# Layer 1 of a cross network in 19 matmul passes instead of 21, with VectorE's products at other places

## The reference, cut to what matters

```python
for W in filters:            # (39*39, 128), (39*128, 128), (39*128, 128)
    z = jnp.einsum('bfd,bgd->bfgd', x0, xk).reshape(b, f * g, d)
    cur = jnp.einsum('bpd,pm->bmd', z, W)
    outs.append(cur)
    xk = cur
z = jnp.sum(jnp.concatenate(outs, axis=1), axis=-1)    # (512, 384)
h = jnp.concatenate([z, dense_ctx], axis=1)
h = jnp.maximum(h @ W_top1 + b_top1, 0.0)
h = jnp.maximum(h @ W_top2 + b_top2, 0.0)
y = h @ W_top3
```

## Time and profile before

| | us |
|---|---|
| median of 2 runs (680.06 to 683.67) | 681.87 |
| the profiled execution, own time | 676.92 |
| its span, first to last instruction | 674.9 |
| busy in that span: TensorE matmul | 636.6 |
| VectorE | 565.5 |
| GpSimd | 533.3 |
| ScalarE | 374.1 |
| first matmul of layer 2 of tile 0 starts at | 45.27 |

### The profile page before, as it was taken

How to read it: one execution, slowest core, us unless ns; L and a number is a source line. 1 busy time by engine, 2 the same in 40 slices (tenths; PEclk the granted TensorE clock), 3 DMA queues, 4 the chain that set the end, 5 groups by cost and what they waited for, 6 DMA issues and landing times.

```text
span 674.9 us, 11454 instructions
## 1 busy us (share of the span) xinstructions
PE 636.6 (94%) x2900; PEld 504.6 (75%) x2900; DVE 565.5 (84%) x1934; ACT 374.1 (55%) x1129; POOL 533.3 (79%) x528
## 2 busy tenths in 40 slices
PE   3388999999999999999999999999999999999998
PEld 1256667777778788888878888888878888887867
DVE  4468888979899898989789898989879898988760
ACT  0445464646556574747467564746557474755431
POOL 6757879999999999998879999897969988574420
PEclk9999999999999999999999999999999999999989
DMA  9535642203241313113230322204031221200000
GB/s 185 112 70 140 211 117 68 62 6 89 40 110 18 98 29 81 44 29 95 43 85 8 84 44 66 60 10 113 10 88 37 63 62 41 81 0 1 2 0 1
DMA packets 79940, 42.25 MB, mean 63 GB/s; under 512 B 56721, under 2 KB 64721, under 8 KB 79746
## 3 DMA queue, kind: packets, MB, share of 16 engines
q1 hardware_dynamic: 67246, 35.85, 20.7%
q10 hardware_dynamic: 7380, 4.38, 3.2%
q0 software_dynamic: 5248, 1.29, 1.9%
HBM read 39.52 MB, written 1.94 MB: 61 GB/s over the span
## 4 chain that ended last, share of the span: by engine, by line
PE 68%; POOL 14%; DVE 5%; issue 5%; SPq 3%; ACT 2%; DMA 2%; POOLq 0%; DVEq 0%
PE y L900 16%; PE y L902 15%; PE y L901 15%; DVE scaled L802 4%; POOL emb_quads L481 4%; PE side L907 4%; PE late L918 4%; PE acc L882 3%; PE acc L877 3%; PE acc L876 3%; POOL sum L514 2%; POOL z_parts L499 2%; POOL sum L507 2%; ACT scaled L594 2%; PE y L918 2%
## 5 line engine op out<-in xcount | busy, mean ns | idle before, releaser
L802 DVE SCALAR_TENSOR_TENSOR scaled<-y,x_rows,scaled 128x128 f32<-128x128 f32 x1728 | 465.4, 341 | 63.4 <-ACT scaled L594 51.7
L594 ACT ACTIVATE scaled<-y,x_rows 128x128 f32<-128x128 f32 x768 | 218.9, 367 | 221.0 <-PE y L902 220.9
L900 PE MATMUL y<-w_hi,x_parts 128*128 128x512 f32 (+1 forms) x640 | 280.5, 438 | 9.5 <-DVE scaled L802 3.4
L902 PE MATMUL y<-w_hi,x_parts 128*128 128x512 f32 (+1 forms) x640 | 248.1, 388 | 0.0
L901 PE MATMUL y<-w_lo,x_parts 128*128 128x512 f32 (+1 forms) x640 | 247.6, 387 | 0.0
L481 POOL DMA_INDIRECT emb_quads<-in_small_tables_dram,quad_rows x144 | 139.2, 967 | 27.4 <-issue 15.6
L900 PEld LDWEIGHTS y<-w_hi,x_parts 128*128 128x128 f32 x640 | 120.6, 188 | 49.6 <-DVE scaled L802 23.0
L499 POOL TENSOR_TENSOR z_parts<-z,z_parts 117x512 fp32r<-117x512 f32 (+1 forms) x95 | 123.3, 1298 | 29.3 <-ACT z_parts L553 28.5
L902 PEld LDWEIGHTS y<-w_hi,x_parts 128*128 128x128 f32 x640 | 120.1, 188 | 24.9
L901 PEld LDWEIGHTS y<-w_lo,x_parts 128*128 128x128 f32 x640 | 121.0, 189 | 20.9 <-issue 2.6
L514 POOL TENSOR_TENSOR sum<-sum,scaled 128x512 f32<-128x512 f32 x63 | 81.7, 1296 | 26.5 <-DVE scaled L802 25.3
(11 more groups left out here) (94 smaller groups left out, 376.2 us busy)
## 6 DMA issues: line engine op xcount, KB each, us to landing
z<-x_turned SPq DMA_DIRECT2D x311, 78.0 KB
x_three<-x_turned SPq DMA_DIRECT2D x48, 78.0 KB
x_turned<-emb_quads SPq DMA_DIRECT2D x156, 8.0 KB
w_sb<-in_w_dram SPq DMA_DIRECT2D x1, 2496.0 KB, 9.6
emb_quads<-in_small_tables_dram,quad_rows POOLq DMA_INDIRECT x144, 2.4
s_sb<-in_w_dram ACTq DMA_DIRECT2D x12, 160.0 KB, 5.3
x_turned<-emb_singles SPq DMA_DIRECT2D x89, 2.0 KB
x_turned<-emb_quads SPq DMA_DIRECT2D x64, 2.0 KB
```

Source lines behind the costliest of these rows:

```text
L594: done = act.activation(scaled[:, k % 2, BY_ACT.index(j), i * M:(i + 1) * M], y2[n % RING][:, i * M:(i + 1) * M], ACT.Copy, scale=x0_rows[ ...
L802: dve.scalar_tensor_tensor(part, y2[n % RING][:, i * M:(i + 1) * M], x0_f, part, ALU.mult, ALU.add).then_inc(terms_in, 1)
L900: pe.matmul(dst, x1_hi[:, t % 2, cols], hi, start=True, stop=False)
L902: pe.matmul(dst, x1_lo[:, t % 2, cols], hi, start=False, stop=True).then_inc(y_ready, 1)
```

## The change

**Layer 1 in 19 passes.** The 780 products are laid out anew. Chunks 0 to 3 get 11 more rows each (rows 117 to 127: the pairs of the last 11 fields with fields shifted by 7 to 10), loaded for all four chunks by one DMA (`more_rows`, semaphore `more_in`), and chunks 4 and 5 get 7 and 8 rows. The shifts 7 and 8 in chunk 2 lose these rows (`MOVED`) and hold pairs of the last ones there. What is left are 19 pairs. They stand three times in chunk 6, and `third_sb`, a column of ones on some rows and zeros on the others, makes the split in such a way that one pass does all three: rows 0 to 38 hold the values with the high filter, rows 39 to 77 the low parts with the high filter, and the rows up to 105 the values with the low filter. So six chunks have three passes and the last has one. The filter's rows are brought into the new places by 22 DMAs from SBUF to SBUF on ScalarE's queue (`filter_pieces`), at the start.

**More DMAs.** `pieces(c)` gives 3, 3, 7, 3, 4, 4 and 6 DMAs for the seven chunks (20 in all before), `three` has a fourth one, and `more_rows` is one: 12 more for a tile on SyncE's queue. `more_rows` comes behind the rows of chunk 3, that is behind `quarters`; the product of chunk 0 waits for it.

**Places.** `PLAIN` is chunk 3 alone. From tile 4 on (`EARLY_FROM`) the products stand at `PRODUCTS_AT` (chunk 0 at slot 28 and chunk 1 at slot 32 of tile `u - 2`, then 1, 6, 10, 15 and 20 of tile `u - 1`), the gathers start 24 slots ahead instead of 14, and `three_ps` is filled at slot 26 instead of 38. `rows` moves from slot 30 to 24, the sum of the maps from 36 to 38.

```diff
+EARLY_AHEAD = 24
 C0 = 7
-TURNS = F // 2 + 1
-PLAIN = (1, 3, 5)
+FULL = 3 * F
+MORE = P - FULL
+MORE_CHUNKS = 4
+MORE_ROW = 7
+MOVED = {7: (21, 7), 8: (20, 8)}
+PLAIN = (3,)
 CHUNKS_AT = (0, 4, 8, 12, 16, 20, 24)
+EARLY_FROM = 4
+PRODUCTS_AT = (-12, -8, 1, 6, 10, 15, 20)
+SUM_AT = 38
-ROWS_AT = 30
+ROWS_AT = 24
 THREE_AT = 38
+EARLY_THREE_AT = 26
...
+def pieces(c):
+    if c == C0 - 1:
+        return [x for r in range(3) for x in ((F * r, 18, 10), (F * r + 19, F, 9))]
+    found = []
+    for r in range(3):
+        shift = 3 * c + r
+        if shift in MOVED:
+            a, n = MOVED[shift]
+            found += [(F * r, shift, a), (F * r + a, F, n), (F * r + a + n, shift + a + n, F - a - n)]
+        else:
+            found.append((F * r, shift, F))
+    if c >= MORE_CHUNKS:
+        a, n = MOVED[c - MORE_CHUNKS + 7]
+        found.append((FULL, a, n))
+    return found
...
+def product_at(t, s):
+    for u in (t + 1, t + 2):
+        places = FIRST_CHUNKS_AT if u == 1 else CHUNKS_AT if u < EARLY_FROM else PRODUCTS_AT
+        at = s - SLOTS * (u - 1 - t)
+        if u < TILES and at in places:
+            return u, places.index(at)
+    return None
...
-        first = (u - 2) * SLOTS - GATHER_AHEAD
+        first = (u - 2) * SLOTS - (EARLY_AHEAD if u >= EARLY_FROM else GATHER_AHEAD)
...
+        def more_rows(queue, u):
+            x = x0_dram[u, MORE_ROW:MORE_ROW + MORE, :]
+            queue.dma_start(z[FULL:P, 0:MORE_CHUNKS, :],
+                            bass.AP(x.tensor, x.offset, [[COLS, MORE], [COLS, MORE_CHUNKS], [1, COLS]])).then_inc(more_in, 16)
...
+                sp.dma_start(x0_three[FULL:P, u % 2, :], x0_dram[u, F - MORE:F, :]).then_inc(three_in[u % 2], 16)
...
                     if c == 2 and u > 0:
                         quarters(u)
+                    if c == MORE_CHUNKS - 1 and u > 0:
+                        more_rows(sp, u)
...
             def product(u, c):
                 if c == 0:
                     dve.wait_ge(three_up, u + 1)
+                    dve.wait_ge(more_in, 16 * (u + 1))
                 dve.wait_ge(a_in[c], rounds(c, u))
...
-                pe.wait_ge(z_hi_in, split(n))
-                pe.matmul(acc0[:, :], w0_hi[0:k, c, :], z_hi[0:k, s, :], start=c == 0, stop=False)
-                pe.matmul(acc0[:, :], w0_lo[0:k, c, :], z_hi[0:k, s, :], start=False, stop=False)
+                last = c == C0 - 1
+                if not last:
+                    pe.wait_ge(z_hi_in, split(n))
+                    pe.matmul(acc0[:, :], w0_hi[0:k, c, :], z_hi[0:k, s, :], start=c == 0, stop=False)
+                    pe.matmul(acc0[:, :], w0_lo[0:k, c, :], z_hi[0:k, s, :], start=False, stop=False)
...
-                pe.matmul(acc0[:, :], w0_hi[0:k, c, :], z_lo[0:k, s, :], start=False, stop=c == C0 - 1).then_inc(z_done, 1)
+                weights = w0_lo if last else w0_hi
+                pe.matmul(acc0[:, :], weights[0:k, c, :], z_lo[0:k, s, :], start=False, stop=last).then_inc(z_done, 1)
```

More of the change, by code:

```diff
@@ L146, in dve_terms, with filter_pieces @@
     return n // BANKS * per_block + sum(len(fields_of(j)) for j in range(n % BANKS + 1) if j not in BY_ACT)
-def turns(c):
-    return min(3, TURNS - 3 * c)
-def depth(c):
-    return F * turns(c)
+def pieces(c):
[13 more added lines that the diff above has]
+    return found
+def depth(c):
+    if c == C0 - 1:
+        return 2 * F + 28
+    return P if c < MORE_CHUNKS else FULL + pieces(c)[-1][2]
+def filter_pieces():
+    last, moved = C0 - 1, 2
+    for c in (0, 1, 3, 4, 5):
+        yield c, 0, c, 0, FULL
+    at = 0
+    for shift, row in ((7, 21), (8, F + 20)):
+        a, n = MOVED[shift]
+        start = F * (shift - 6) + a
+        yield moved, at, moved, at, start - at
+        yield moved, start, last, row, n
+        at = start + n
+    yield moved, at, moved, at, FULL - at
+    for c, row in enumerate((28, F + 28, F + 9, 10)):
+        yield c, FULL, last, row, MORE
+    for c, shift in ((4, 7), (5, 8)):
+        a, n = MOVED[shift]
+        yield c, FULL, moved, F * (shift - 6) + a, n
+    for r in range(3):
+        yield last, F * r, last, 0, 10
+        yield last, F * r + 19, last, F, 9
 def chunk_at(u, s, lag):
@@ L368, in rounds @@
         def rounds(c, u):
-            return 16 * turns(c) * (u + 1)
+            return 16 * len(pieces(c)) * (u + 1)
         def turned_rows(queue, u, c):
-            for r in range(turns(c)):
-                shift = 3 * c + r
-                queue.dma_start(z[F * r:F * r + F, c, :], x0_dram[u, shift:shift + F, :]).then_inc(a_in[c], 16)
+            for at, row, n in pieces(c):
+                queue.dma_start(z[at:at + n, c, :], x0_dram[u, row:row + n, :]).then_inc(a_in[c], 16)
+        def more_rows(queue, u):
+            x = x0_dram[u, MORE_ROW:MORE_ROW + MORE, :]
+            queue.dma_start(z[FULL:P, 0:MORE_CHUNKS, :],
+                            bass.AP(x.tensor, x.offset, [[COLS, MORE], [COLS, MORE_CHUNKS], [1, COLS]])).then_inc(more_in, 16)
         def load_filter(queue, j):
@@ L432, in _ @@
             sp.dma_start(ids_sb[:, 1:GROUPS, :], ids[P:B, :].rearrange("(g p) f -> p g f", p=P)).then_inc(rest_ids_in, 16)
+            for j in (0, 1):
+                load_filter(sp, j)
             for u in range(TILES):
@@ L649, in _ @@
             act.dma_start(bt1_sb[:, :], bt1).then_inc(dense_in, 16)
-            for j in range(W1_PIECES):
+            for j in (2, 3):
                 load_filter(act, j)
+            act.wait_ge(clear, 2)
             act.wait_ge(w0_sum, 1)
-            copy(w0_hi[:, :, :], w0_raw).then_inc(w0_hi_in, 1)
+            for c, at, there, row, n in filter_pieces():
+                act.dma_start(w0_raw[at:at + n, c, :], w0_both[row:row + n, there, :]).then_inc(w0_in_rows, 16)
             act.wait_ge(dense_in, 48)
@@ L667, in _ @@
             act.wait_ge(stored[0], 16 * STORES)
+            more_rows(act, 0)
             turned_rows(act, 0, 0)
@@ L697, in _ @@
                         three(1)
-                    if t + 2 < TILES and s == THREE_AT:
+                    if t + 2 < TILES and s == three_at(t + 2):
                         three(t + 2)
@@ L852, in _ @@
                         add_dense(t // TPG - 1)
-                    c = chunk_at(t + 1, s, 0)
-                    if c is not None and not plain(C0 * (t + 1) + c):
-                        product(t + 1, c)
+                    due = product_at(t, s)
+                    if due is not None and not plain(C0 * due[0] + due[1]):
+                        product(*due)
                     if t + 1 < TILES and s == ROWS_AT:
@@ L859, in _ @@
                         x1_low(t + 1)
-                    if t + 1 < TILES and s == x1_at(t + 1) + 2:
+                    if t + 1 < TILES and s == SUM_AT:
                         sum_x1(t + 1)
```

40 lines of the change are left out of this document (32 added, 8 removed).

## The result

The changed kernel takes 808.7 us (807.3 to 810.1), the one before 681.9: a ratio of 1.188 (95% interval 1.182 to 1.193), 127 us slower. The forecast was 773 us, the range 738 to 800.

What follows compares the result with a forecast made beforehand. TensorE's passes were taken to bound tiles 4 to 14, with SyncE's queue deciding the change. 676.9 - 5.1 + 59 + 21.3 + 16 = 768 us, plus 5 for the median, gave 773 us, range 738 to 800.

Steps and rivals of the forecast that it cites:

- The wait for `more_rows`: Tiles 4 to 15: VectorE's product of chunk 0 waits for these late rows, 62.8 us in sum, 59 counted.
- The pattern by the last gather's slot: From tile 4 on: VectorE's wait is 8.1 us for slot 15, 4.2 for slot 11, 1.9 for slot 8.
- What is hidden of a wait: TensorE runs on until bank 33 while VectorE waits, hiding 0.3 us each time, 12 x 0.3 = 3.6 us.
- The start: Before tile 0: quarters issued 4.1 us later, ScalarE's copies 2 to 6 us later, all inside 21.3 us.
- the same 21.3: Tiles 1 and 2: SyncE's late queue moves the rows of tile 2 from 87.75 to 109.1, costing 21.3 us.
- The clock: TensorE falls to half speed behind six waits of 4.9 us and more, 2.7 us each, 16 us.
- The bound of 7 us: If the ramp is under 1% of a typical span, TensorE's clock loss is at most 7 us here.
- The passes: Tiles 4 to 14: TensorE's passes set the time, so two fewer per tile at 0.23 us save 5.1 us.
- The places: New slots of products and gathers: no term of their own in the sum beyond VectorE's wait for rows.
- rival (b): Tiles 1 to 4: closer gathers, late ScalarE and late queue add up to 15 us, about 795; chance 0.14.
- one fall of the clock: One drop of TensorE to half speed behind a wait of 4.9 us or more, counted at 2.7 us.

Runs made afterwards that it cites:

- the last experiment: The kernel before, with only the loads of the layer 3 and top-layer weights moved on SyncE's queue from tile 1 to 3: 677.5 us, 0.993.

## Why the prediction was right in kind and short in size

**The wait for `more_rows`.** Right, and shown by two experiments that change SyncE's issues alone: without it 105 us are back, with 5.7 us less ahead of it 71. The pattern by the last gather's slot came as written. The term was mis-sized: 78.9 us for 62.8. From gather to product it is 20.6 us (tile 10) to 21.5 (tile 8) instead of 19.8: landing 2.45 instead of 1.9, and for tile 8 a gap in the rows of chunk 2 on top. And VectorE is at the place 0.4 us earlier than the row of before had it. With 12 waits, one us too few in the chain is 12 us; here the five waits of slot 15 are some 2 us longer each than forecast, those of slot 8 0.4 shorter. A landing taken from one row of an early tile was one weak number, chain prices without a gap in them the other.

**What is hidden of a wait.** 0.3 us were taken off; in tile 8 it is 0.7 (9.56 of 10.2), in tile 10 1.1 (4.31 of 5.4).

**The start.** This step failed: "ScalarE's 22 DMAs for the filter (9 us at 0.41) ... come 2 to 6 us later, and stay under the same 21.3". They take 17.8 us, twice the price, and what stands behind them in the queue is more than the copies: ScalarE's stores, on which all of tile 0 waits. `three` of tile 0 is 13.6 us late, where the prediction had it in its old place. The rest of the chain was right: the product of chunk 0 of tile 2 comes 33.2 us late (120.9 against 87.75) and not 21.3, and these 12 us are what tile 0's delay adds (`three` of tile 2 starts at 104.5 for 92.6, and 16.4 us later the product, for 16.5). From there to the first matmul of tile 2 it is 41.4 us, before 33.4. The prediction had nothing for these 8 us; 10 us of tile 1 ran at the lower clock, and the rest is open. The price 0.41 was that of DMAs from DRAM of 39 rows; the trace of before had none from SBUF to SBUF, and its 16 loads of the second filter at the start stood at 0.64, which would have been nearer. With the filter laid out before, 7 us of the 15.3 go. Moving the eight loads back from SyncE's queue changed nothing that can be seen. About 4 us are what two executions of the same instructions differ by at the start (45.3 and 49.2), so no experiment here settles the remaining 4 by its single profile. Without the 22 DMAs SyncE's twelve stores still take 13.46 us instead of 9.51, but in the last experiment they take 14.38 with nothing changed. The cause of this half stays open; the 11 additional DMAs of tile 0's rows are a guess that wasn't tried alone.

**The clock.** Right in kind: the clock fell behind the long waits, and holding it over five of them took 8.6 us off their tiles. It is 1.7 us for a stall, not 2.7. Whether the 16 us were right in sum isn't shown, since the other stalls were not held, nor what the 17 us at the lower clock in tile 0 cost beside the waits there. The bound of 7 us that the Trainium skill's sentence gives (TensorE: Matmul & The Clock Gate, part 1) looks too low here, though no run settles it: the held kernel is 10 us faster by the medians with 58 of the 109 us at the lower clock still there, but of the 8.6 us of the five tiles two other tiles took back 3.7.

**The passes.** "In these tiles, 4 to 14, the time is TensorE's passes" was right in the main at the old places and not at the new. At the old places 22 passes gave 3.7 us of 5.1, at the new ones nothing was left of them (419.6 against 419.3), and taking 22 more gave 2.1. A pass is recorded for 0.39 us and the next starts after 0.23, so they overlap by 0.16 us, and stalls of up to that length between two passes don't show in a busy share of 100%.

**The places.** The prediction gave them no cost but the wait. They cost 2 us in tiles 4 to 14 with 21 passes, 4 us with 19, and more in one of the early tiles: tile 2 took 41 to 43 us with them and 37.3 without, or, in the three kernels with own rows and the top weights in tile 1, tile 1 took 47 to 50 and tile 2 36 us. That the gathers of two tiles meet there is a likely cause that no run tried alone. It was rival (b)'s; how much of it is in the changed kernel isn't shown.

**The sum again** by what was measured: start +15.3, tiles 0 to 3 +43.9, tiles 4 to 14 +70.9. The forecast's terms for the first two (21.3, the waits of tiles 4 and 5, one fall of the clock) are some 36 us for 59.2, those for the last some 55 for 70.9, so the early part was short by 23 us and the later by 16. Tiles 4 to 14 take 70.3 us more than in the kernel with own rows; 62.7 of them are the waits for tiles 6 to 15, and 7.7 the clock less what is hidden of the waits, which these runs don't separate.

## What to carry to other kernels

When a step moves forward in an engine's order, its waits move with it; list each one and follow the queue that feeds it back to the last thing that can't be earlier, in issues times price. A wait shared by several loads should be split so that the first user waits for its own only: here three more DMAs per tile beat one shared one by 105 us. And putting right a queue that is late early in a kernel can be worth more than passes in its steady part: one line that moves loads two tiles later gave 4.9 us by itself. The new layout at its best, with this line, own rows and the filter laid out before the launch in it, is 3.3 us under the kernel before, so of the layout itself no gain is shown. Hold a combined change against each of its parts, not only against the start.

## What the runs showed of the hardware

The 22 DMAs from SBUF to SBUF cost ScalarE's queue 0.81 us each to issue, where one from DRAM to SBUF of 39 rows of 2 KB costs SyncE's 0.41 (`more_rows`, 11 rows of four pieces, 0.35). They stand at the start, right behind eight loads from DRAM that cost the same queue 1.06 us each, so whether the source or the place makes the price isn't separated. After a stall of 9.6 us TensorE's passes start 0.43 us apart instead of 0.23, and 39 small float32 matmuls of zeros over 8.9 us keep the clock at the higher level. Two executions with the same instructions up to the first matmul of layer 2 reach it at 45.3 and 49.2 us. Over the 38 executions of the kernel before that ran beside the experiments the time goes with the granted clock: 679.8 us in the mean of the seven at 0.992, 684.6 of the eight at 0.985.
